# A fused eight-layer kernel: the second attention's keys and values finished in the time-warping stage

## What is computed

```python
x = x + time_warping(ctx, layernorm(x))       # per batch: distances, cost table, backtrack, scatter-add of ctx rows
x = x + gated_ffn(layernorm(x))
x = x + attention_2(layernorm(x), ctx)        # 16 heads of 16; queries and keys are rotated by place
# attention_2:
q = rope(x @ Wq.T); k, v = split(ctx @ Wkv.T); k = rope(k)
out = softmax(q @ k.T) @ v                    # rope(a) = a*cos + swapped_pairs(a)*sin
x = x + out @ Wo.T
```

## Time and profile before

| | us |
|---|---|
| median of 3 runs | 2587.84 (2584.61 to 2589.24) |
| the profiled execution | 2591.72 |
| its span in the profile | 2589.9 |
| busy: PE / DVE / ACT / POOL | 2011.9 / 1664.3 / 1115.9 / 1012.3 |

### The profile page before, as it was taken

How to read it: one execution, slowest core, us unless ns; L and a number is a source line. 1 busy time by engine, 2 the same in 40 slices (tenths; PEclk the granted TensorE clock), 3 DMA queues, 4 the chain that set the end, 5 groups by cost and what they waited for, 6 DMA issues and landing times. The chain is left out here.

```text
span 2589.9 us, 40039 instructions
## 1 busy us (share of the span) xinstructions
PE 2011.9 (78%) x13073; PEld 1624.0 (63%) x13073; DVE 1664.3 (64%) x5395; ACT 1115.9 (43%) x3119; POOL 1012.3 (39%) x955
## 2 busy tenths in 40 slices
PE   6985898699559948866999847777777778765996
PEld 4664797699538835555999835555555555544663
DVE  5764111588972258843111189999999999964773
ACT  3552232555221114431333246666666666641443
POOL 3310453200000046403555446666666666606430
PEclk9996899655779979967999966667667666567997
DMA  2111575410210012124464230000000000000112
GB/s 88 65 55 58 215 244 182 121 21 1 81 37 1 0 45 73 57 69 145 136 212 156 80 96 9 1 9 9 1 9 9 1 1 1 1 7 26 42 47 77
DMA packets 91587, 161.09 MB, mean 62 GB/s; under 512 B 18366, under 2 KB 69718, under 8 KB 83414
## 3 DMA queue, kind: packets, MB, share of 16 engines
q0 software_dynamic: 23808, 85.50, 9.6%
q1 hardware_dynamic: 67576, 73.06, 9.0%
HBM read 194.38 MB, written 33.33 MB: 88 GB/s over the span
## 5 line engine op out<-in xcount | busy, mean ns | idle before, releaser
L555 DVE MATCH_REPLACE8 l3a_left<-l3a_top,l3a_left 128x256 f32<-128x256 f32 x768 | 308.9, 410 | 0.0
L548 DVE MAX8 l3a_top<-l3a_left 128x8 f32<-128x256 f32 x768 | 286.0, 415 | 0.0
L365 POOL TENSOR_TENSOR l3a_prob<-l3a_expd,l3a_rest 128x512 f32<-128x512 f32 x128 | 162.5, 1270 | 230.3 <-ACT l3a_rest L445 230.0
L270 PE MATMUL l3a_psT<-all_ident,l3a_prob 128*128 128x128 f32 x512 | 123.5, 387 | 163.9 <-POOL l3a_prob L365 163.9
L288 PE MATMUL l3a_psO<-l3a_probT,l3a_vp 128*128 128x128 f32 x1024 | 216.0, 377 | 28.8 <-ACT l3a_probT L461 28.8
L288 PEld LDWEIGHTS l3a_psO<-l3a_probT,l3a_vp 128*128 128x128 f32 x1024 | 185.5, 271 | 81.7 <-ACT l3a_probT L461 48.3
L270 PEld LDWEIGHTS l3a_psT<-all_ident,l3a_prob 128*128 128x128 f32 x512 | 83.8, 196 | 186.6 <-POOL l3a_prob L365 186.1
L352 POOL TENSOR_TENSOR l3a_kept<-l3a_raw_sc,l3a_mone 128x512 f32<-128x512 f32 x128 | 163.3, 1276 | 49.1 <-ACT l3a_raw_sc L429 48.9
L1465 ACT ACTIVATE l2f_hT<-l2f_psH,l2f_wt 128x128 f32<-128x128 f32 x312 | 89.2, 369 | 216.3 <-PE l2f_psH L1397 216.3
L445 ACT ACTIVATE l3a_rest<-l3a_left,l3a_nmax 128x256 f32<-128x256 f32 x256 | 116.1, 502 | 151.5 <-DVE l3a_left L555 150.8
L932 POOL TENSOR_SCALAR l2a_xn<-all_x,l2a_nmean,all_rstd 128x256 f32<-128x256 f32 x16 | 8.8, 562 | 433.6 <-DVE all_rstd L106 433.6
(11 more groups left out here) (528 smaller groups left out, 4715.5 us busy)
## 6 DMA issues: line engine op xcount, KB each, us to landing
o_at<-l0a_oraw SPq DMA_DIRECT2D x16, 256.0 KB, 2.0
l0a_osum<-o_at SPq DMA_DIRECT2D x32, 128.0 KB
kv_at<-dtw_kv SPq DMA_DIRECT2D x8, 512.0 KB, 2.8
o_at<-l2a_oraw SPq DMA_DIRECT2D x16, 256.0 KB, 2.0
l2a_osum<-o_at SPq DMA_DIRECT2D x32, 128.0 KB
l2f_yb<-rows_y SPq DMA_DIRECT2D x8, 512.0 KB, 7.4
o_at<-l3f_oraw SPq DMA_DIRECT2D x16, 256.0 KB, 2.0
l3f_osum<-o_at SPq DMA_DIRECT2D x32, 128.0 KB
```

What stands on the lines that cost most here:

```text
L270: mm = nc.tensor.transpose(psT[u % 2][:, kc, e, :], prob[:, u % 4, e, kc * P:kc * P + P], ident[:])
L365: nc.gpsimd.tensor_tensor(prob[:, u % 4, :, :], expd[:, u % 2, :, :], rest[:, u % 2, :, :], ALU.subtract).then_inc(picked, 1)
L548: ins = nc.vector.max(top[:, e, eight], rows[:, e, :] if r else scores[:, e, :])
L555: ins = nc.vector.match_replace(out=rows[:, e, :], in_to_replace=top[:, e, eight], in_values=rows[:, e, :] if r else scores[:, e, :], imm_ ...
```

## The change

The finished forms are made in the time-warping stage. For the swapped neighbours the keys are projected a second time with a weight matrix whose columns are exchanged in pairs (`L2_wk_pairs`), so no exchange on VectorE is needed for them. GpSimd turns the keys (three `tensor_tensor` of 512 elements a batch), ScalarE parts them into `k2` and spreads the values into `vd`. `kv_at` grows from 512 KB to 1 MB a batch, and the second attention loads `k2` and `vd` from it ready for use; its `kf`, `vraw`, the memset of `vd`, `read_v`, the keys' `exchange` and `k_parted` go (the other users of the function keep theirs).

```diff
 # second attention, SP queue
-                    if b >= 2:
-                        sp.wait_ge(k2_set, b - 1)
-                        sp.wait_ge(v_ev, b - 1)
-                    sp.dma_start(kf[:, b % 2, :, :], of[:, 0]).then_inc(kv_in[b % 2], 16)
-                    sp.dma_start(vraw[:, b % 2, :, :], of[:, 1]).then_inc(kv_in[b % 2], 16)
+                    if b >= 3:
+                        sp.wait_ge(s2_done, 16 * (b - 2))
+                        sp.wait_ge(pv_ps, 2 * (b - 2))
+                    sp.dma_start(k2[:, b % 3, ...], kv_at[b, :, 0:4 * S]).then_inc(kv_in[b % 3], 16)
+                    sp.dma_start(vd[:, b % 3, ...], kv_at[b, :, 4 * S:]).then_inc(kv_in[b % 3], 16)
...
             for y in range(2 * B):
-                if given and y % 2 == 0 and y // 2 + 4 < B:
+                if given and kv_at is None and y % 2 == 0 and y // 2 + 4 < B:
                     load(y // 2 + 4)
+                if kv_at is not None and y % 2 == 0 and 3 <= y // 2 + 2 < B:
+                    load(y // 2 + 2)
                 realign(y)
 # second attention, TensorE, first step of a batch
                     pe.wait_ge(qd_set, b + 1)
-                    pe.wait_ge(k2_set, b + 1)
+                    if kv_at is None:
+                        pe.wait_ge(k2_set, b + 1)
+                    else:
+                        pe.wait_ge(kv_in[b % 3], 32 * (b // 3 + 1))
 # time-warping stage, SP queue
             for i, b in enumerate(KV_ORDER):
-                sp.wait_ge(kv_ev, 2 * (i + 1))
-                sp.dma_start(kv_at[b]..., kv[:, i % 2, :, :, :]).then_inc(kv_out[i % 2], 16)
+                sp.wait_ge(kv_ev, 3 * (i + 1))
+                sp.dma_start(kv_at[b, :, 4 * S:], vd[:, i % 2, ...]).then_inc(kv_out[i % 2], 16)
                 if i < 4:
                     sp.dma_start(aT[:, i, :, :], ctxT[...]).then_inc(a_again[i], 16)
+                sp.wait_ge(k_parted, i + 1)
+                sp.dma_start(kv_at[b, :, 0:4 * S], k2[:, i % 2, ...]).then_inc(kv_out[i % 2], 16)
 # time-warping stage, TensorE: 3 projections a batch (keys, keys with pairs swapped, values), one kv_ps each
-                    pe.wait_ge(kv_ev, 2 * (i - 1))
+                    pe.wait_ge(kv_ev, 3 * (i - 1))
-            pe.wait_ge(kv_ev, 2 * B)
+            pe.wait_ge(kv_ev, 3 * B)
 # time-warping stage, GpSimd, new
+            nc.gpsimd.memset(vd[:]..., 1.0).then_inc(vd_one, 1)
+            pool.wait_ge(kv_w_in, 96)
+            for i in range(B):
+                pool.wait_ge(kv_ev, 3 * i + 2)
+                for w, wave in enumerate((cosT, sinT)):
+                    nc.gpsimd.tensor_tensor(kx[:, i % 2, w, :, :], kx[:, i % 2, w, :, :], wave..., ALU.mult).then_inc(k_waved, 1)
+                pool.wait_ge(k_waved, 2 * (i + 1))
+                nc.gpsimd.tensor_tensor(kx[:, i % 2, 0, :, :], kx[:, i % 2, 0, :, :], kx[:, i % 2, 1, :, :], ALU.add).then_inc(k_turned, 1)
 # time-warping stage, ScalarE, new
+            def parted(i):
+                act.wait_ge(k_turned, i + 1)
+                if i >= 2:
+                    act.wait_ge(kv_out[i % 2], 32 * (i // 2))
+                for e in range(2):
+                    ins = nc.scalar.activation(k2[:, i % 2, e, :, :], kx[:, i % 2, 0, :, :], ACT.Identity, bias=even[:, 2 + e:3 + e], scale=even[:, e:e + 1])
+                ins.then_inc(k_parted, 1)
             for i in range(B):
+                # copies: kx from psD (keys), kx from psT (keys, swapped), then vd from psB in two, each with its wait
...
+                if i:
+                    parted(i - 1)
+            parted(B - 1)
```

More of the change, by code:

```diff
@@ L622, in paired_attention @@
         kvT = s.sb("kvT", [P, 2, DC, S]) if ctxT is not None else xnT
-        vraw = s.sb("vraw", [P, 2, QT, D]) if kv_at is not None else None
-        qf, kf = s.sb("qf", [P, 2, DC, S]), s.sb("kf", [P, 2, DC, S])
+        qf = s.sb("qf", [P, 2, DC, S])
+        kf = s.sb("kf", [P, 2, DC, S]) if kv_at is None else None
         qd, q2 = s.sb("qd", [P, 2, 2, DC, S]), s.sb("q2", [P, 2, 2, DC, S])
@@ L655, in paired_attention @@
             s.sem(n) for n in ("q_in", "k_in", "v_in", "w_in", "bqs_set", "nmean_set", "x_norm", "bo_in", "vd_one", "nm_zero"))
-        kv_in, o_out, o_in = ([s.sem(f"{n}{p}") for p in range(2)] for n in ("kv_in", "o_out", "o_in"))
+        kv_in = [s.sem(f"kv_in{p}") for p in range(2 if kv_at is None else 3)]
+        o_out, o_in = ([s.sem(f"{n}{p}") for p in range(2)] for n in ("o_out", "o_in"))
         xT_ps, q_ps, k_ps, v_ps, nm_ps, pv_ps, out_ps = (
@@ L660, in paired_attention @@
             s.sem(n) for n in ("xT_ev", "q_ev", "k_ev", "v_ev", "qd_set", "k2_set", "q2_set"))
[L661 to L662 removed]
+        q_shuf, q_cos, q_sin, q_turn = (s.sem(n) for n in ("q_shuf", "q_cos", "q_sin", "q_turn"))
         s1_done, max_done, s2_done, exp_done, o_ev, inv_set, o_set, x_done = (
@@ L831, in values @@
                 pe.wait_ge(exp_done, 8 * (y + 1))
-                if c == 0:
+                if c == 0 and kv_at is None:
                     pe.wait_ge(v_ev, b + 1)
@@ L972, in k_parted @@
             def k_parted(b):
-                if rope is not None:
-                    turn(b, 1, kf, k_shuf, k_shuf, k_cos, k_sin, k_turn)
-                else:
-                    pool.wait_ge(k_ev, b + 1)
+                pool.wait_ge(k_ev, b + 1)
                 if b >= 3:
@@ L1008, in _ @@
             q_parted(0)
-            k_parted(0)
+            if kv_at is None:
+                k_parted(0)
             pool.wait_ge(w_in, 16 * n_w)
@@ L1020, in _ @@
                     q_parted(b + 1)
-                if t == 2 and b + 1 < B:
+                if t == 2 and b + 1 < B and kv_at is None:
                     k_parted(b + 1)
@@ L1117, in read_v @@
             def read_v(b):
-                if kv_at is None:
-                    dve.wait_ge(v_ps, b + 1)
-                else:
-                    dve.wait_ge(kv_in[b % 2], 32 * (b // 2 + 1))
+                dve.wait_ge(v_ps, b + 1)
                 if b >= 3:
@@ L1125, in read_v @@
                         dve.wait_ge(rg_pv, b - 2)
-                src = (bank_of("v", b)[:] if kv_at is None else vraw[:, b % 2, :, :]).rearrange("p t (h d) -> p t h d", d=DK)
+                src = bank_of("v", b)[:].rearrange("p t (h d) -> p t h d", d=DK)
                 dst = vd[:, b % 3, :, :, 0:DK]
@@ L1240, in _ @@
                 nc.vector.memset(mrow[:, 1, :, :].rearrange("p e n -> p (e n)"), 0.0).then_inc(m_zero, 1)
-            nc.vector.memset(vd[:].rearrange("p b k h m -> p (b k h m)"), 1.0).then_inc(vd_one, 1)
-            dve.wait_ge(vd_one, 1)
+            if kv_at is None:
+                nc.vector.memset(vd[:].rearrange("p b k h m -> p (b k h m)"), 1.0).then_inc(vd_one, 1)
+                dve.wait_ge(vd_one, 1)
             dve.wait_ge(q_in, 16 * n_q)
             if rope is not None:
-                exchange(0, 0, qf, q_ev, q_shuf, q_sin, q_turn)
-                exchange(0, 1, kf, k_ev if kv_at is None else None, k_shuf, k_sin, k_turn)
+                exchange(0)
             dve.wait_ge(w_in, 16 * n_w)
-            read_v(0)
+            if kv_at is None:
+                read_v(0)
             dve.wait_ge(nm_zero, 1)
@@ L1258, in _ @@
                 if rope is not None and t == 1 and b + 1 < B:
-                    exchange(b + 1, 0, qf, q_ev, q_shuf, q_sin, q_turn)
-                if rope is not None and t == 2 and b + 1 < B:
-                    exchange(b + 1, 1, kf, k_ev if kv_at is None else None, k_shuf, k_sin, k_turn)
+                    exchange(b + 1)
                 if n < NQ:
                     row_max(n, (2, 3))
-                if t == 2 and b + 1 < B:
+                if t == 2 and b + 1 < B and kv_at is None:
                     read_v(b + 1)
@@ L1674, with alignment @@
 TOP = 512.0
-def alignment(nc, x, ident, rstd, mean, consts, ctx, ctxT, dist, kv_w, kv_at):
+def alignment(nc, x, ident, rstd, mean, consts, ctx, ctxT, dist, kv_w, kv_at, rope, evens):
     with Scope(nc, "dtw") as s:
```

107 lines of the change are left out of this document (63 added, 44 removed).

## The result

The changed kernel takes 2598.56 us (median of 7 runs, 2591.54 to 2601.91), the kernel before 2586.72 (median of 7, 2581.26 to 2589.24): a ratio of 1.0044, 95% interval 1.003 to 1.0058. It is slower by more than 0.2%, and 3.6 us above the forecast of 2595 and inside its own range of 2590 to 2602.

A forecast was written before the change was run, and what follows sets the result against it. VectorE alone was taken to bound the time-warping walk, while no engine is full in the second attention. +25 from GpSimd blocking and -17.6 from the attention gave +7.4 us: 2595, forecast's own range 2590 to 2602, overall 2574 to 2606.

The forecast's parts named there:

- VectorE alone bounds the walk, TensorE and ScalarE are covered: Time-warping stage: VectorE sets its end; added projections (15 us) fit TensorE's idle 30.71 us, ScalarE's 3.3 us a batch too.
- GpSimd blocks VectorE at 1.05 us each, +25: Walk of the time-warping stage: each of 24 GpSimd tensor_tensor pushes VectorE back 1.05 us, 25 us more in all.
- The lower bound: Walk: blocking of 0.9 us per GpSimd operation, 21.7 us in all, read from two VectorE copies beside GpSimd.
- The upper bound: Walk: VectorE pays the whole duration of each GpSimd operation, 24 x 1.27 = 30.5 us.
- as all those of the walk have: Walk: claimed that all its VectorE operations have two inputs in SBUF, like the operation seen held up by GpSimd.
- 5.5 us each at batches 0 and 1, 1.9 at the next: Second attention: scores_1 starts 5.5 us earlier at batch 0, another 5.5 at batch 1; batch 1 itself gains 1.9.
- t = 2 of 3.99 us, loads issued at +7.8, scores at +14.5: Second attention: step t = 2 falls to 3.99 us; timed from scores_1 of t = 1, loads landing at +14.4 delay the scores.
- A gain of 4.7 us from batches 3 to 7: Second attention: with late loads, a gain of 0.9 us a period, 4.7 in five, instead of 11.2.
- and a period of 19.9: Second attention, batches 3 to 7: 14.5 + 5.38 us a period, with a kv_in wait of about 1.2 us.
- Loads in time: Rival, chance 0.2: second attention gains 24 us, blocking as in the forecast, kernel -3 to +6 us; periods of 18.6.
- The chain itself late: Rival, chance 0.15: key chain ends late, TensorE waits for kv_ev or ScalarE for kv_out; +12 to +22 us.
- No blocking: Rival, chance 0.2: GpSimd blocks VectorE not at all or a third as much; -24 to -10 us, 2564 to 2578.

The follow-up runs named there:

- the second profile: The changed kernel run once more, unchanged: 2588.52 us in its one run, walk 81.6, second attention 208.0.
- four profiles: One attention code: changed kernel twice, without GpSimd's turn, turn in the feed-forward; attention 214.1, 208.0, 213.6 and 206.4 us.
- before's three: Kernel before, unchanged and with 15 or ten added GpSimd operations on tiles of their own; attention 226.9, 223.9 and 225.0 us.
- the turn in the feed-forward: Changed kernel with GpSimd's turn and parting of the keys moved to the gated feed-forward: 2570.61 us, ratio 0.9926 to the kernel before.
- the three kernels that made them so: Changed kernel with four buffers (2581.77 us), with three buffers and keys' load first (2579.91), with four buffers and turn in feed-forward (2557.19).

## Why the prediction came out right

- **VectorE alone bounds the walk, TensorE and ScalarE are covered.** Right: `dv` still released line 1855, after 21.00 us of idle time. Without GpSimd's operations all other added work left the walk at 59.2.
- **GpSimd blocks VectorE at 1.05 us each, +25.** Right in kind, high in size: 0.93 each, +22.4. The lower bound, read from two copies (0.9, 21.7), was nearly exact. The upper bound was too high because it charged the whole GpSimd operation: when VectorE's begins, 1.02 to 1.21 us of it are left, and some 0.15 us at its end are hidden as well. The forecast's 1.05 lay between the two bounds with no row for it. Its "as all those of the walk have" isn't exact either: the copy ahead of the rounds has one input, and it too grew, from 0.32 to 1.20 us. The Trainium skill, page "SBUF — State Buffer", section "SBUF: two separate sides", lets the one block for the whole instruction of the other. The trace agrees: VectorE with two SBUF inputs is held until the GpSimd operation that reads SBUF is through (all 24), and isn't beside a memset (0.00) or with an input in PSUM (0.47 as ever). What the prediction made of it, 24 whole operations or 30.5 us, doesn't follow: 22.4 was measured, since only the part of a GpSimd operation that is still to run is waited for.
- **5.5 us each at batches 0 and 1, 1.9 at the next.** Right in sum: `scores_1` starts 5.6, 11.8 and 13.0 us earlier in its stage at batches 0, 1 and 2, where 5.5, 11 and 12.9 were foreseen. That the third agrees to 0.1 us is luck. TensorE was at its half level in part of this stretch of this execution (clock 0.50 at 30 to 36 us into the stage); in the second profile, at the full level there, batch 2 starts 15.0 us earlier, and between the means of four profiles and of before's three it is 14.2.
- **t = 2 of 3.99 us, loads issued at +7.8, scores at +14.5.** Right as to the steps and the issue: 3.98 and +7.8. The scores came later than foreseen, at +14.7 to +16.0 in this profile. TensorE's idle time there was foreseen at 1.2 and was 1.12, 1.75, 2.13, 2.96 and 2.64 us. The first of these agrees by luck: in the step before it (7.15 us) TensorE was at the half level and so was late itself; in the two profiles of this attention that have the full level there the same wait is 1.95 and 2.17 us.
- **A gain of 4.7 us from batches 3 to 7.** This is the term that was mis-sized. From batch 2 to the end the profile shows none (13.0 earlier at batch 2, 12.8 at the end). The step of the prediction that failed is "and a period of 19.9": it has the wait at 1.2 us throughout and no clock in it. The load landed at +14.6 to +15.9 and not at +14.4, and TensorE would have been ready at +12.9 (read where the loads are in time) and not at +13.2, so the wait, against a TensorE that is ready at +12.9, was 1.8 to 3.0 us. In this execution the clock also fell after the three longest, so that t = 0 took 6.5 to 7.6 us instead of 5.4. The periods became 20.1 to 22.6, 21.3 in the mean; in the profile with the turn in the feed-forward, where t = 0 stayed at 5.4, they are 20.5 in the mean, so the wait alone makes some 0.6 a period. Why the values of batch 6 take 7.6 us from issue to landing in all four profiles, where most others take 6.3 to 6.8, stays open. A single profile exaggerates the miss: in the second one the stage was 208.0 us, 18.9 less than the 226.9 of the earlier trace rows. Between the means of the four profiles and of before's three the attention gains 14.8 us, 14.2 of them before batch 2 and 0.6 after it, where 12.9 and 4.7 were foreseen.
- **The rivals.** Loads in time: no, but the three kernels that made them so show what it is worth, 196.2, 196.7 and 196.6 us. That is 29 below the mean of before's three, where 24 were foreseen; the period was 18.4 and not 18.6, and before's own three profiles lie 3 us apart. The chain itself late: no. No blocking: no.
- **The errors partly cancel.** +22.4 instead of +25, and -12.8 instead of -17.6 in the profiled execution. With the attention's mean gain of 14.8 the sum is +7.6, next to the forecast's +7.4; that it comes so near is luck, since both terms were too large by some 3 us. The medians lie 11.8 us apart, and the 4 us between that and the sum are of the size of the kernel's own spread.

## What to carry to other kernels

Work given to an idle GpSimd isn't free if VectorE is the bound and reads only SBUF there: count the GpSimd operations that read SBUF times the measured 0.93 us (two inputs, 128x512), and look for a stretch in which VectorE has room or reads PSUM: with the same operations in it the feed-forward took 150.6 us, where the profiles without them show 150.0 to 151.3. When a load moves, read its place in the queue and every semaphore it waits for: one that belongs to another tensor can make it late, and three stalls of 2.1 to 3.0 us on TensorE were followed by a lower clock that cost 1.2 to 2.2 us more each. A change that loses as a whole may hold two gains; take its parts one by one before dropping it.

## What the runs showed of the hardware

- The price of the contention is per pair of operations and doesn't grow with the VectorE operation's length: +0.95 us on one of 5.17 and on a scan of 10.22, +0.94 on one of 0.47. All 24 held operations of the changed kernel end 0.14 to 0.15 us before GpSimd's end plus their own undisturbed length.
- A one-input GpSimd `tensor_scalar` of 128x512 costs VectorE 0.27 us, a two-input operation of the same size 0.93, though alone they are 0.77 and 1.27 us long: the ratio of the prices is 3.4, that of the lengths 1.6. The rows explain it by what is still to run when VectorE's operation begins, 0.38 to 0.44 and 1.02 to 1.10 us beside the small rounds, of which some 0.15 us are hidden; the number of inputs isn't needed for it. A one-input operation as long as a two-input one wasn't tried.
- An operation of VectorE with one tensor input, all in SBUF, is held up as well: the copy in the walk, 0.32 us before and 1.20 after (687.00), and the normalisation of the feed-forward with the turn beside it, by the view of its line (duration least, median and most).

```profile
L2216 DVE TENSOR_SCALAR l1f_xn<-all_x,all_mean,all_rstd x16: 403/408/1429, 764.7 to 884.1; 128x256 f32<-128x256 f32 x8, 128x256 f32 x8
```

At most 1.43 us instead of 0.41, which is the most in the kernel before. VectorE has room for it there.
- TensorE's clock came down after a stall of 2.96 us in one execution and not after one of 3.02 in another; between them the same attention took 206.4 to 214.1 us. A single profile of this stage tells the effect of an edit only to some 8 us, and the medians were needed. In the kernel before the clock came down after idle time of 1.67 us in one batch and not after 1.66 us in the batch before.
